# Two-tensor sums folded into neighbouring operations, and token-shifted copies written by GpSimd inside the producing stage

## The reference

```python
def shift_token(t):                    # half of the features come from one token earlier
    t1, t2 = jnp.split(t, 2, axis=-1)
    t2 = jnp.pad(t2, ((0, 0), (1, 0), (0, 0)))[:, :-1]
    return jnp.concatenate([t1, t2], axis=-1)

def _layer(x, ...):                    # twice in every l0_ffn
    h = shift_token(x)
    ...                                # window attention on h, 8 heads of 64
    x = x + o @ wo
    h = shift_token(x)
    h = layer norm(h) * lg + lb
    h = h @ w1 + b1;  a, g = jnp.split(h, 2, axis=-1);  h = a * gelu(g)
    return x + h @ w2 + b2

# l1_ffn ends in:  _layer_norm(tgt + tgt2, gamma, beta), which is then added to x
```

## Time and profile before

| | us |
|---|---|
| three runs | 6434.0, 6409.55, 6407.12 |
| their median | 6409.55 |
| the profiled execution | 6412.5 |
| its span in the trace | 6410.7 |
| PE busy in the span | 5549.0 (87%) |
| DVE busy | 3373.6 (53%) |
| ACT busy | 3372.2 (53%) |
| POOL busy | 2511.9 (39%) |

### The profile page before, as it was taken

How to read it: one execution, slowest core, us unless ns; L and a number is a source line. 1 busy time by engine, 2 the same in 40 slices (tenths; PEclk the granted TensorE clock), 3 DMA queues, 4 the chain that set the end, 5 groups by cost and what they waited for, 6 DMA issues and landing times. The chain is left out here.

```text
span 6410.7 us, 126831 instructions
## 1 busy us (share of the span) xinstructions
PE 5549.0 (87%) x46005; PEld 3283.8 (51%) x46005; DVE 3373.6 (53%) x4109; ACT 3372.2 (53%) x5089; POOL 2511.9 (39%) x1721
## 2 busy tenths in 40 slices
PE   6876888888887998998898998998898998778998
PEld 2432555555544654553444554653445775445776
DVE  4557999999945554553444554553552112553112
ACT  4545888888834553554444553554343434443443
POOL 1223999999924542660224642561320000000000
PEclk8997999999998999999999999999998999998999
DMA  0002010111111110110001110110000000000000
GB/s 40 1 0 79 29 33 29 33 30 32 30 42 35 40 32 20 46 40 0 1 0 34 41 33 20 41 44 27 1 0 7 0 0 0 0 0 0 0 0 13
DMA packets 119694, 137.07 MB, mean 21 GB/s; under 512 B 31712, under 2 KB 85088, under 8 KB 118240
## 3 DMA queue, kind: packets, MB, share of 16 engines
q1 hardware_dynamic: 119520, 134.75, 7.5%
HBM read 46.55 MB, written 12.58 MB: 9 GB/s over the span
## 5 line engine op out<-in xcount | busy, mean ns | idle before, releaser
L2367 POOL TENSOR_TENSOR arena<-arena,wbig 128x1024 f32<-128x1024 f32 x512 | 1192.1, 2484 | 106.6 <-DMA wbig<-scratch_b 100.4
L2354 DVE TENSOR_TENSOR_SCAN arena<-banks,arena 128x1024 f32<-128x1024 f32 x512 | 1140.4, 2278 | 68.4 <-ACT banks L2298 51.3
L768 POOL TENSOR_TENSOR X<-X,Z 128x1536 f32<-128x1536 f32 x2 | 9.5, 4758 | 1583.0 <-ACTq L761 1583.0
L601 DVE TENSOR_REDUCE arena<-banks 128x4 f32<-128x1024 f32 (+1 forms) x384 | 401.7, 1046 | 433.0 <-PE banks L435 305.3
L989 ACT ACTIVATE arena<-banks,wbig 128x512 f32<-128x512 f32 x512 | 350.3, 688 | 514.8 <-PE banks L946 504.3
L1511 POOL TENSOR_TENSOR arena<-arena 128x512 f32<-128x512 f32 x256 | 354.6, 1385 | 594.8 <-DMA arena<-arena 594.8
L2298 ACT ACTIVATE banks<-banks 128x1020 f32<-128x1020 f32 x512 | 518.1, 1012 | 108.8 <-PE banks L2219 101.4
L1021 DVE SCALAR_TENSOR_TENSOR arena<-banks,arena 128x128 f32<-128x128 f32 x512 | 144.1, 344 | 818.7 <-PE banks L930 818.7
L2303 ACT COPY arena<-banks 128x1024 f32<-128x1024 f32 x512 | 520.8, 1017 | 50.3 <-POOL arena L2367 29.7
L547 ACT ACTIVATE Y<-banks 128x2048 f32<-128x2048 f32 x192 | 305.7, 1592 | 408.8 <-PE banks L471 311.6
L930 PEld LDWEIGHTS banks<-wbig,arena 128*128 128x128 f32 x4096 | 475.0, 192 | 53.6 <-issue 53.6
(11 more groups left out here) (301 smaller groups left out, 10729.2 us busy)
## 6 DMA issues: line engine op xcount, KB each, us to landing
arena<-arena SPq DMA_DIRECT2D x1024, 64.0 KB, 2.0
wbig<-scratch_d SPq DMA_DIRECT2D x512, 16.0 KB, 1.7
wbig<-scratch_b SPq DMA_DIRECT2D x64, 128.0 KB, 2.2
wbig<-scratch_c SPq DMA_DIRECT2D x64, 128.0 KB, 2.1
arena<-Z SPq DMA_DIRECT2D x64, 128.0 KB, 2.1
wbig<-in_l_ffn SPq DMA_DIRECT2D x1, 4185.0 KB, 12.9
X<-in_x SPq DMA_DIRECT2D x2, 2048.0 KB, 14.6
wbig<-in_l_ffn SPq DMA_DIRECT2D x1, 3879.5 KB, 11.8
```

The source lines that it names most:

```text
L601: dve.tensor_reduce(to, mbank[:, :, :, 0:keys], AX_X, ALU.max).then_inc(dve_m.sem, 1)
L2354: dve.tensor_tensor_scan(own, line(decay_bank[n % 2]), own, 0.0, ALU.mult, ALU.add)\
L2367: pool.tensor_tensor(four(h[par][:, m * 1024:m * 1024 + 1024]), four(us[n % 2]), Bs[par].unsqueeze(1).to_broadcast([128, 4, SEQ]), ALU.mult)\
```

## The change

A helper `shifted_parts` names the two copies that make a shifted piece: the lower 64 partitions straight, the upper 64 one token later in each sequence. All `add_stage` and `shift_stage` calls and both functions go.

- `norm_stage` gets `add_to` (the bias operation also adds a tensor) and `shifted` (POOL writes the shifted copy of each tile once DVE has made it).
- `gated_mlp_stage` gets `shifted`, and where `dst` is not `add_to`, DVE first adds `add_to` into `dst` and then the output of the MLP; where they are the same, a semaphore step is skipped.
- `window_attention_stage`: POOL writes the shifted copy of sequence `b - 2` between `rotary` and `low` of trip `b`, for `b` from 2 on, with a wait on its own last sum before and a wait on its own last copy after; the last two sequences are copied at the end.
- The block that waits for the second load of `X` stands ahead of the last MLP of `l0_attn_a`, no longer behind it.

```diff
+def shifted_parts(dst, src, at, width):
+    def per_batch(ap, rows):
+        return ap[rows, bass.ds(at, width)].rearrange("p (b t) -> p b t", t=SEQ)
+    low, high = slice(0, 64), slice(64, 128)
+    return [(dst[low, bass.ds(at, width)], src[low, bass.ds(at, width)]),
+            (per_batch(dst, high)[:, :, 1:SEQ], per_batch(src, high)[:, :, 0:SEQ - 1])]
...
 # norm_stage, DVE, where there is a bias
-                    dve.tensor_scalar(columns(outs[0][0], t), pre[t % bufs], outs[0][2], None, ALU.add)\
-                        .then_inc(dve_s.sem, 1)
+                    if add_to is None:
+                        last = dve.tensor_scalar(columns(outs[0][0], t), pre[t % bufs], outs[0][2], None, ALU.add)
+                    else:
+                        last = dve.scalar_tensor_tensor(out=columns(outs[0][0], t), in0=pre[t % bufs],
+                                                        scalar=outs[0][2], in1=columns(add_to, t), op0=ALU.add,
+                                                        op1=ALU.add)
+                    last.then_inc(dve_s.sem, 1)
+        if shifted is not None:
+            @block.gpsimd
+            def _(pool):
+                pool.memset(shifted[64:128, 0:TOKENS].rearrange("p (b t) -> p b t", t=SEQ)[:, :, 0:1], 0.0)
+                for t in tiles:
+                    pool.wait_ge(dve_s.sem, dve_s.at(0, f"z{t}"))
+                    for to, own in shifted_parts(shifted, outs[0][0], t * TILE, TILE):
+                        pool.tensor_copy(to, own)
...
 # gated_mlp_stage, DVE
             with dve.Fori(0, TILES) as i:
+                if dst is add_to:
+                    dve_s.skip(dve, i, "both")
+                else:
+                    dve.tensor_tensor(dst[:, tok(i, TILE)], dst[:, tok(i, TILE)], add_to[:, tok(i, TILE)], ALU.add)\
+                        .then_inc(dve_s.sem, 1)
...
                 dve.wait_ge(pe_s.sem, pe_s.at(i, "out"))
+                dve.wait_ge(dve_s.sem, dve_s.at(i, "both"))
                 dve.scalar_tensor_tensor(out=dst[:, tok(i, TILE)], in0=obank,
-                                         scalar=b_out if b_out is not None else 1.0, in1=add_to[:, tok(i, TILE)],
+                                         scalar=b_out if b_out is not None else 1.0, in1=dst[:, tok(i, TILE)],
...
+        if shifted is not None:
+            @block.gpsimd
+            def _(pool):
+                for i in range(TILES):
+                    pool.wait_ge(dve_s.sem, dve_s.at(i, "sum"))
+                    for to, own in shifted_parts(shifted, dst, i * TILE, TILE):
+                        pool.tensor_copy(to, own)
...
 # window_attention_stage, POOL
-            def trip(b, par):
+            def shift_sum(b):
+                pool.wait_ge(dve_y.sem, dve_y.at(b, "sum"))
+                for to, own in shifted_parts(shifted, y, b * SEQ, SEQ):
+                    pool.tensor_copy(to, own).then_inc(pool_h.sem, 1)
+
+            def trip(b, par, back):
                 for g in groups:
                     rotary(b, g)
+                if back:
+                    pool.wait_ge(pool_f.sem, pool_f.at(b, "add3"))
+                    shift_sum(b - 2)
+                    pool.wait_ge(pool_h.sem, pool_h.at(b - 2, "high"))
                 for g in groups:
                     low(b, par, g)
...
+            pool.wait_ge(pool_f.sem, pool_f.at(BATCH - 1, "low3"))
+            shift_sum(BATCH - 2)
+            shift_sum(BATCH - 1)
...
 # l1_ffn
-    norm_stage(k, f"{name}_last", k.H, [(k.Z, w["gamma"], w["beta"])], True, "eps5")
-    add_stage(k, f"{name}_add", k.Z, k.X)
+    norm_stage(k, f"{name}_last", k.H, [(k.X, w["gamma"], w["beta"])], True, "eps5", add_to=k.X)
...
 # l0_ffn
-    norm_stage(k, f"{name}_ln", k.X, [(k.Y, None, None)], True, "eps5")
+    norm_stage(k, f"{name}_ln", k.X, [(k.Y, None, None)], True, "eps5", shifted=k.H)
...
-        shift_stage(k, f"{s}_shift1", k.Y, k.H)
-        window_attention_stage(k, f"{s}_attn", k.H, k.Y, lw, tables)
-        shift_stage(k, f"{s}_shift2", k.Y, k.H)
+        window_attention_stage(k, f"{s}_attn", k.H, k.Y, lw, tables, k.H)
         norm_stage(k, f"{s}_norm", k.H, [(k.Z, lw["lg"], lw["lb"])], True, "eps5")
         gated_mlp_stage(k, f"{s}_mlp", k.Z, [128, 128, 85], lw["w_lin"], lw["w_act"], lw["b_lin"], lw["b_act"],
-                        lw["w_out"], ACT.Gelu, GELU_SET, k.Y, k.Y, lw["b_out"])
-    add_stage(k, f"{name}_add", k.Y, k.X)
+                        lw["w_out"], ACT.Gelu, GELU_SET, k.Y, k.X if layer else k.Y, lw["b_out"],
+                        shifted=None if layer else k.H)
...
 # l0_attn_a
-    gated_mlp_stage(k, f"{name}_mlp", k.H, [128] * 4, w["w_lin"], w["w_act"], None, None, w["w_out"], ACT.Silu,
-                    SILU_SET, k.Y, k.Y, None)
     with k.nc.Block() as block:
         @block.sync
         def _(sp):
             sp.wait_ge(again.sem, again.at(16))
-    add_stage(k, f"{name}_add", k.Y, k.X)
+    gated_mlp_stage(k, f"{name}_mlp", k.H, [128] * 4, w["w_lin"], w["w_act"], None, None, w["w_out"], ACT.Silu,
+                    SILU_SET, k.Y, k.X, None)
```

More of the change, by code:

```diff
@@ L132, in _, with norm_stage @@
                 sp.wait_ge(landed[n].sem, landed[n].at(16))
-def norm_stage(k, name, src, outs, center, eps):
+def shifted_parts(dst, src, at, width):
[4 more added lines that the diff above has]
+            (per_batch(dst, high)[:, :, 1:SEQ], per_batch(src, high)[:, :, 0:SEQ - 1])]
+def norm_stage(k, name, src, outs, center, eps, add_to=None, shifted=None):
     nc = k.nc
@@ L676, in _, with gated_mlp_stage @@
                                              op1=ALU.add).then_inc(dve_s.sem, 1)
-def gated_mlp_stage(k, name, src, widths, w_lin, w_act, b_lin, b_act, w_out, func, table, add_to, dst, b_out):
+def gated_mlp_stage(k, name, src, widths, w_lin, w_act, b_lin, b_act, w_out, func, table, add_to, dst, b_out,
+                    shifted=None):
     nc = k.nc
@@ L688, in gated_mlp_stage @@
     act_s = Steps(k, "gates", act_steps, TILES)
-    dve_s = Steps(k, "hidden", dve_steps + ["sum"], TILES)
+    dve_s = Steps(k, "hidden", ["both"] + dve_steps + ["sum"], TILES)
     k.arena.reset()
@@ L1054, with window_attention_stage @@
 TINY_SCALE = 2.0 ** 20
[L1057 to L1079, removed]
+def window_attention_stage(k, name, src, y, w, tables, shifted):
     nc = k.nc
@@ L1098, in window_attention_stage @@
     pool_f = Steps(k, "sides", [f"{s}{f}" for f in groups for s in ("sin", "add")] + [f"low{f}" for f in groups], BATCH)
+    pool_h = Steps(k, "shifted", ["low", "high"], BATCH)
     swapped = [Count(k, f"swapped{g}", 64 * BATCH) for g in groups]
@@ L1507, in _ @@
             pool_f.prime(pool)
+            pool_h.prime(pool)
             def rotary(b, g):
@@ L1521, in low @@
                                    ones[:, 0:1].to_broadcast([128, TILE]), ALU.mult).then_inc(pool_f.sem, 1)
-            def trip(b, par):
+            def shift_sum(b):
[3 more added lines that the diff above has]
+            def trip(b, par, back):
                 for g in groups:
                     rotary(b, g)
+                if back:
+                    pool.wait_ge(pool_f.sem, pool_f.at(b, "add3"))
+                    shift_sum(b - 2)
+                    pool.wait_ge(pool_h.sem, pool_h.at(b - 2, "high"))
                 for g in groups:
                     low(b, par, g)
-            with pool.Fori(0, BATCH // 2) as ii:
+            for par in range(2):
+                trip(par, par, False)
+            with pool.Fori(1, BATCH // 2) as ii:
                 for par in range(2):
-                    trip(ii * 2 + par, par)
+                    trip(ii * 2 + par, par, True)
+            pool.wait_ge(pool_f.sem, pool_f.at(BATCH - 1, "low3"))
+            shift_sum(BATCH - 2)
+            shift_sum(BATCH - 1)
         @block.sync
```

## The result

The changed kernel takes 6464.31 us (median of 4 runs, 6461.35 to 6481.57) against 6409.44 us before: a ratio of 1.0082, 95% interval [1.0052, 1.0113]. It is 55 us slower. The forecast was 6402 us and no difference; the time lies above the range (6384 to 6442). The profiled execution has a span of 6462.3 us, 51.6 more than before.

What follows compares the result with a forecast made beforehand. It took attention trips to be a loop through POOL's chain ahead of L1519, add and shift stages to lie wholly on the path. -32.0 + 1.5 - 12.0 - 13.6 - 14 + 62.7 = -7.4 from 6409.55: 6402 us, range 6384 to 6442.

Steps and rivals of the forecast that it cites:

- The adds: Five add stages removed at 6.40 us each, -32.0; three-input DVE operations in the two closing norms, +1.5.
- The shifts: Eight shift stages removed: four behind a norm or MLP save 3.0 us each, four behind an attention 3.4 each.
- PE's clock at the starts: Seven norm starts behind removed stages gain clock as PE idles less, 2.0 us each: -14 (0 to -20).
- POOL's copies inside: Two copies and their waits ahead of the first low lengthen 56 attention trips by 1.12 us each: +62.7.
- a wait for its own last sum: In each attention trip, POOL's wait ahead of the copies costs 0.16 us; the wait behind them was priced the same.
- lost overlap of 0.04: The first low operation (L1519) no longer overlaps POOL's last sum: 0.04 us of the 1.12 per trip.
- My upper bound of 1.4: High case for the POOL addition per attention trip, 1.4 us each: +78 in place of +62.7.
- The half clock: Rival: PE's clock falls in half of the 56 attention trips, 1.6 us per fall, +45, total 6447; chance 0.14.
- around L1196 PE has no other idle time: Argument against the rival of clock falls in attention: PE's idle share is lower here than around L1749.
- 1.78 us that I forecast: PE's stall before L1196 in each attention trip was to grow from 0.66 to 1.78 us.
- The signs that I named for the slow side: Clock of 0.50 behind L1196 in many trips, or copies well over 0.40 us, would show the forecast too fast.

Runs made afterwards that it cites:

- experiment 3: The kernel before with the add stages gone and their sums folded in, all eight shift stages kept: 6378.13 us, ratio 0.995.
- experiments 5 and 7: 5: copies behind the low operations, only POOL's two waits ahead: 6372.25 us. 7: changed kernel plus one POOL operation between copies and first low: 6553.57 us.
- experiment 1: The changed kernel with POOL's two shifted copies moved behind the four low operations of the trip: 6363.38 us, ratio 0.9918.
- experiment 4: The changed kernel with 12 unused bf16 products put into PE's stall before maxima(b+1, 0): 6422.79 us, ratio 1.0018.

## Why the prediction was wrong

**The adds, -32.0 + 1.5: right.** The sums alone gave 31 us (experiment 3) against 30.5 and some 3 of clock.

**The shifts, -12.0 and -13.6: right.** Copies of 512 columns take 0.61 us and the pair of 256 columns 0.85, as worked out from the earlier trace rows; the end of an attention shows the saving of 3.4 us. Behind the first norm it is 2.8 us and not 3.0 (7.61 us from the last product of DVE to the first of the attention on PE before, 4.82 after).

**PE's clock at the starts, -14: right in sum.** The norms behind the attentions gained 2.9, 2.4, 2.1 and 3.0 us on PE (18.45, 17.93, 17.66 and 18.53 down to 15.53 each), 10.4 in all. The four behind the adds (the fourth of which I hadn't counted) went from 18.45, 16.90, 18.30 and 17.22 to 15.42, 17.11, 16.83 and 18.36, 3.1 in all. That the sum of 13.5 meets the forecast is in part luck: the first four gave 2.6 each where I had 2.0, and of the others one gave 3.0, one 1.5, and two lost 0.2 and 1.1. Altogether the part outside the attentions was forecast at -70.1 us and came to -73.4.

**POOL's copies inside, +62.7: mis-sized.** The place, the mechanism and the number of trips were right, and so was the duration of each copy. The term that failed is "a wait for its own last sum, 0.16 us by the gap that the same kind of wait leaves before L1514", used for both waits. They cost 0.34 and 0.25 us, 0.59 where I had 0.32. The row that I took the price from has a wait with at most two register steps of the sequencer behind it. The new waits exposed four and three such steps, among them those of the low operations, which had run under the last sum before (experiments 5 and 7). The pair of copies took 0.84 and not 0.76. With the lost overlap of 0.04 this makes 1.47 us. The trip grew by 1.53; the remaining 0.06 is also in the trip of experiment 1, with nothing ahead of the low operations, and its cause is open. In 56 trips that is 85.7 us and not 62.7. My upper bound of 1.4 did not hold it either.

**The half clock: put apart where it should have been added.** I had it as a rival with 0.14, at 1.6 us per fall, from the earlier trace rows. It fell behind 26 of 56 stalls and cost 1.4 us each, 36 us; filling the stall took the falls away (experiment 4). Two judgements failed. First, "around L1196 PE has no other idle time" was held for enough protection; the table shows no fall at 1.1 us and 26 in 56 at 2.2. Second, I took the price of the waits and the clock for separate cases, but they have one cause: the stall that was mis-sized by 0.4 us is also what decides the falls. At the 1.78 us that I forecast, a fall would have been rare (4 of 56 at 1.75). The sum of both, 85.7 + 36 = 122, stands against 125.0 in the trace.

**What would have shown it.** The signs that I named for the slow side were 0.50 behind L1196 in many trips, or copies well over 0.40 us. The first appeared and the second did not, and the stall came out at 2.2 us and not at the 1.8 that I named. The trace of the kernel before already held the register steps of the low operations, under the last sum.

Left open: whether the copies could stand between the sums and the low operations without waits. That wasn't tried, because POOL's copies cover 64 partitions and its other operations 128, and the page GPSIMD Engine Reference of the Trainium skill, section "Instruction dispatch", says that consecutive POOL instructions are no barrier between its eight cores. No run here shows what happens then.

## What to carry to other kernels

Before work is put on an engine that is "idle most of the time", find the one instruction of it that others wait for, and put the work behind that one: the same two copies with their waits cost 86 us ahead of POOL's first low operation and almost nothing behind its last. Price each new wait by what it exposes: read from the trace which register steps of the sequencer run under the operation ahead today, and add those that the wait puts behind it (here 0.25 to 0.34 us and not 0.16). And where a delay lengthens a stall of PE, ask at once what the clock does at the new length of the stall: here that second price was some 36 us on top of 86, and twelve useless products per trip removed it.

## What the runs showed of the hardware that was not expected

- PE at 0.50 of its clock behind stalls of 2.2 us, in a stage in which it is otherwise busy: 26 of 56, against 4 of 56 at 1.75 us and none at 1.09.
- A stage that no kernel here touches, the experts of the first `l1_ffn`, took 504.6 us in one profiled execution and 520.3 in another, at granted clocks of 1.00 and 0.97. With 10 runs, experiment 4 spread over 19 us. Differences under 20 us between kernels are better read from the trips and stages of the traces than from the medians.
- A wait for POOL's own last operation left from 0.09 to 0.34 us of idle time, by how many register steps of its sequencer it exposes. Without such a wait they run under the operation ahead.
- In four of the five add stages of the kernel before, DVE's 2560 columns (L764) took 6.08 to 6.09 us beside POOL's 1536 in 3.41 to 3.42. In the fifth (at 5423.06 us) DVE took 2.82 and POOL 6.10. The two additions started together each time, and the longer one ended 2.7 to 3.3 us behind the other, as if for the most part they ran one after the other. So a stage of 6.1 us held an addition that DVE could do in 2.82. What decides which of the two comes first is open.
